# Second depthwise convolution of a selective-scan layer: tap split between three engines and order of its PSUM banks

## The reference

```python
xin = jnp.einsum('bchw,oc->bohw', x, in_proj_w)
xc = jax.nn.silu(_dwconv(xin, conv2d_w, conv2d_b))     # first depthwise 3x3
x1 = _dwconv(xc, dw_w, dw_b)                           # second depthwise 3x3
x1 = gelu(_layer_norm(x1 over channels, dw_ln_g, dw_ln_b))
offset = x1 @ off_w.T + off_b                          # 8 numbers a pixel
xd = _dcn_sample(xc, offset)                           # bilinear gather at the offsets
...                                                    # scan, layer norm, projection
```

## Time and profile before

| | |
|---|---|
| median of 3 runs | 2626.13 us |
| the profiled execution, its own time | 2632.59 us |
| its span | 2630.7 us |
| mean granted clock of TensorE | 0.934 |

### The profile page before, as it was taken

The page is one execution under the profiler, slowest core; times in us unless marked ns, Lnnn a source line. Parts: engine busy times, 40 slices in busy tenths (PEclk is TensorE's granted clock), DMA queues, the critical chain, the costliest instruction groups (busy, mean ns, idle before and its releaser), DMA issues.

```text
span 2630.7 us, 29183 instructions
## 1 busy us (share of the span) xinstructions
PE 2209.4 (84%) x7671; PEld 1139.9 (43%) x7671; DVE 1954.1 (74%) x3324; ACT 1457.5 (55%) x2268; POOL 1419.7 (54%) x1223
## 2 busy tenths in 40 slices
PE   3898769897978989986988977889899689899788
PEld 2397525343433333332335964454344233333233
DVE  6556746598967999994765667566889499999754
ACT  1743533485765676663346436237677466766532
POOL 2231019387857888872322400475778388888532
PEclk9988879899989999998997988899999799999989
DMA  4000463400000010014720008333000001001145
GB/s 175 1 1 0 150 215 105 167 1 0 0 1 1 17 33 17 16 33 122 236 46 1 0 1 288 117 104 128 0 0 1 2 1 32 17 21 29 51 119 120
DMA packets 131749, 155.96 MB, mean 59 GB/s; under 512 B 4951, under 2 KB 107743, under 8 KB 128247
## 3 DMA queue, kind: packets, MB, share of 16 engines
q1 hardware_dynamic: 131575, 154.00, 19.1%
HBM read 81.69 MB, written 72.29 MB: 59 GB/s over the span
## 4 chain that ended last, share of the span: by engine, by line
PE 42%; DVE 25%; issue 12%; POOL 8%; ACT 7%; DMA 3%; SPq 1%; DVEq 1%; ACTq 0%; POOLq 0%
PE PSUM L2190 7%; POOL BIG L900 6%; PE PSUM L701 6%; PE PSUM L2011 4%; DVE BIG L816 3%; DVE BIG L840 3%; PE PSUM L2246 3%; PE PSUM L2054 3%; PE PSUM L2252 2%; PE PSUM L2068 2%; PE PSUM L2210 2%; DVE BIG L847 2%; DVE PSUM L823 2%; DVE BIG L1082 2%; DVE BIG L861 2%
## 5 line engine op out<-in xcount | busy, mean ns | idle before, releaser
L900 POOL TENSOR_TENSOR BIG<-BIG 128x512 f32<-128x512 f32 x320 | 407.3, 1273 | 108.3 <-DVE BIG L861 86.1
L816 DVE TENSOR_TENSOR BIG<-PSUM,BIG 128x512 f32<-128x512 f32 x576 | 379.1, 687 | 74.1 <-PE PSUM L1010 31.1
L1082 DVE SCALAR_TENSOR_TENSOR PSUM<-BIG,VECS,PSUM 128x1024 f32<-128x1024 f32 x240 | 309.2, 1288 | 43.8 <-PE PSUM L2011 37.4
L742 POOL TENSOR_TENSOR BIG<-TOEP,BIG 128x384 f32<-128x384 f32 x84 | 97.2, 1183 | 342.7 <-DVE BIG L1484 342.7
L1010 PE MATMUL PSUM<-BIG,SELB 120*128 120x512 bf16 x576 | 211.6, 387 | 82.6 <-DVE BIG L816 74.7
L2011 PE MATMUL PSUM<-BIG,WDW 128*128 128x512 f32 x576 | 263.5, 604 | 11.3 <-ACT BIG L1920 11.3
L1718 POOL TENSOR_SCALAR BIG<-BIG,VECS 128x1024 f32<-128x1024 f32 x64 | 181.3, 2845 | 50.6 <-DVE PSUM L1542 50.6
L2190 PE MATMUL PSUM<-BIG 128*128 128x381 f32 (+1 forms) x576 | 190.1, 494 | 15.2 <-DVE BIG L749 15.2
L1016 PE MATMUL PSUM<-BIG,CSTS 128*128 128x512 f32 x384 | 202.4, 609 | 0.0
L1010 PEld LDWEIGHTS PSUM<-BIG,SELB 120*128 120x128 bf16 x576 | 56.0, 98 | 277.4 <-DVE BIG L816 185.1
L2011 PEld LDWEIGHTS PSUM<-BIG,WDW 128*128 128x128 f32 x576 | 108.2, 192 | 141.5 <-issue 126.9
(11 more groups left out here) (362 smaller groups left out, 5366.5 us busy)
## 6 DMA issues: line engine op xcount, KB each, us to landing
spill<-X SPq DMA_DIRECT2D x18, 1024.0 KB, 6.3
back_spill<-BIG SPq DMA_DIRECT2D x32, 576.0 KB, 3.4
X<-x SPq DMA_DIRECT2D x32, 512.0 KB, 7.6
rows_spill<-X SPq DMA_DIRECT2D x64, 256.0 KB, 4.2
out<-BIG SPq DMA_DIRECT2D x64, 256.0 KB, 3.6
BIG<-rows_spill SPq DMA_DIRECT2D x28, 512.0 KB, 5.1
X<-back_spill SPq DMA_DIRECT2D x14, 896.0 KB, 11.7
BIG<-fc SPq DMA_DIRECT2D x8, 1024.0 KB, 9.7
```

The lines of the kernel that those rows point to most:

```text
L742: eng.tensor_tensor(to.rearrange("p (x c r) -> p x c r", x=3, r=WROW), TOEP[:, y].unsqueeze(1).unsqueeze(1).broadcast_to([P, 3, WCH, WROW] ...
L816: dve.tensor_tensor(img(o), img(PSUM[:, (k + q) % 2, :]), pch(c, XBASE, dy, dx), ALU.mult).then_inc(df_p, 1)
L900: pool.tensor_tensor(XS[:, k, :], XS[:, k, :], product_buffer(q), ALU.add).then_inc(df_add, 1)
L1082: return dve.scalar_tensor_tensor(out=rows8(to), in0=strip(c, base, dy, dx), scalar=vc(weights, j), in1=rows8(acc), op0=ALU.mult, op1=ALU.add)
```

## The change

The nine taps are divided anew, and `d2_acc(c)` goes round three pairs of banks (0-1, 2-3, 4-5). GpSimd makes taps 4, 5 and 6, each with a multiplication and an addition of zero in one instruction, with two additions of two tensors; its `d_side` has two buffers. On even strips TensorE makes taps 7 and 8 and VectorE taps 0 to 3; on odd strips TensorE makes tap 8 and VectorE 0, 1, 2, 7 and 3. The centring is written back to the strip's own accumulator, and the offsets of strip c to the banks of strip c+1. VectorE now normalizes strip c-1 after the last tap of strip c and copies the offsets of c-3 before the later taps of c. TensorE makes the offsets of c-2 between centring and mean of c. ScalarE applies the Gelu of c-1 after the exponential of c. `d_xb` has one buffer.

```diff
-DW1_VECTOR, DW2_VECTOR = (4, 5), 6
-DW2_SIDE = (5, 6)
-DW2_FIRST = DW2_VECTOR - 1 + len(DW2_SIDE)
+DW1_VECTOR, DW2_VECTOR = (4, 5), (5, 6)
+DW2_TAPS, DW2_SIDE, DW2_FIRST = ((0, 1, 2, 3), (0, 1, 2, 7, 3)), (4, 5, 6), (7, 8)
+SIDE_STEPS = 2 * len(DW2_SIDE) - 1
...
-            return banks(2 * (c % 2))
-
-        IN, CEN, VAR = banks(6), banks(4), banks(6)
-        OFFS = PSUM[:, 6, 0:8 * 16].rearrange("p (r g) -> p r g", r=8)
+            return banks(2 * (c % 3))
+
+        IN, VAR = banks(6), banks(6)
+        def offs(c):
+
+            return PSUM[:, 2 * ((c + 1) % 3), 0:8 * 16].rearrange("p (r g) -> p r g", r=8)
...
                 def taps(c, first, last):
+                    n = DW2_VECTOR[c % 2]
...
-                        if j == DW2_VECTOR - 2:
-                            dve.wait_ge(d1_part, d2_side_done(pair_d2, c, 2))
-                            dve.tensor_tensor(d2_acc(c), d2_acc(c), d_side, ALU.add).then_inc(d2_tap, 1)
-                        elif j == DW2_VECTOR - 1:
-                            if c >= 2:
-                                dve.wait_ge(d2_cen, half_done(pair_d2, c - 2, 1))
-                            add_tap(dve, c, j - 1, XBASE, "dw_w", d2_acc(c), d_xb[:, c % 2, :]).then_inc(d2_tap, 1)
+                        if j == n - 2:
+                            dve.wait_ge(d1_part, d2_side_done(pair_d2, c, SIDE_STEPS - 1))
+                            dve.tensor_tensor(d2_acc(c), d2_acc(c), d_side[:, c % 2, :], ALU.add).then_inc(d2_tap, 1)
+                        elif j == n - 1:
+                            if c >= 1:
+                                dve.wait_ge(d2_cen, half_done(pair_d2, c - 1, 1))
+                            add_tap(dve, c, DW2_TAPS[c % 2][j - 1], XBASE, "dw_w", d2_acc(c), d_xb).then_inc(d2_tap, 1)
...
                 for c in range(NS):
-                    taps(c, 0, 4)
+                    taps(c, 0, 3)
+                    if c >= 3:
+                        offsets(c - 3)
+                    taps(c, 3, DW2_VECTOR[c % 2])
                     if c >= 1:
                         normal(c - 1)
-                    if c >= 2:
-                        offsets(c - 2)
-                    taps(c, 4, DW2_VECTOR)
                 normal(NS - 1)
+                offsets(NS - 3)
                 offsets(NS - 2)
                 offsets(NS - 1)
...
                 for c in range(NS):
-                    if c >= 1:
-                        pool.wait_ge(d2_tap, d2_taps_done(pair, c - 1, DW2_VECTOR - 2))
+                    if c >= 2:
+                        pool.wait_ge(d2_tap, d2_taps_done(pair, c - 2, DW2_VECTOR[c % 2] - 2))
...
-                    for to, j in zip((d_side, d_tap), DW2_SIDE):
+                    for n, j in enumerate(DW2_SIDE):
                         dy, dx = TAPS[j]
-                        pool.tensor_scalar(rows8(to), strip(c, XBASE, dy, dx), vc("dw_w", j), None, ALU.mult).then_inc(d1_part, 1)
-                    pool.wait_ge(d1_part, d2_side_done(pair, c, 1))
-                    settle(pool)
-                    pool.tensor_tensor(d_side, d_side, d_tap, ALU.add).then_inc(d1_part, 1)
+                        if n >= 1 and (c >= 1 or n >= 2):
+                            pool.wait_ge(d1_part, d2_side_done(pair, c, 2 * n - 2) if n >= 2 else
+                                         d2_side_done(pair, c - 1, SIDE_STEPS - 1))
+                            settle(pool)
+                        pool.tensor_scalar(rows8(d_tap if n else d_side[:, c % 2, :]), strip(c, XBASE, dy, dx), vc("dw_w", j),
+                                           cs("zero")[:, 0:1], ALU.mult, ALU.add).then_inc(d1_part, 1)
+                        if n >= 1:
+                            pool.wait_ge(d1_part, d2_side_done(pair, c, 2 * n - 1))
+                            settle(pool)
+                            pool.tensor_tensor(d_side[:, c % 2, :], d_side[:, c % 2, :], d_tap, ALU.add).then_inc(d1_part, 1)
...
                     act.preload_act_table_set("gelu_and_others")
-                    act.wait_ge(d2_y, strip_done(pair, c))
-                    act.activation(d_y[:, c % 2, :], d_y[:, c % 2, :], ACT.Gelu, bias=vc("dw_ln_b"),
-                                   scale=vc("dw_ln_g")).then_inc(d2_g, 1)
+                    if c >= 1:
+                        gelu(c - 1)
+                gelu(NS - 1)
...
-                    pe.wait_ge(d2_tap, d2_taps_done(pair, c, DW2_VECTOR - 1))
+                    pe.wait_ge(d2_tap, d2_taps_done(pair, c, DW2_VECTOR[c % 2] - 1))
+                    for h in range(2):
+                        half = slice(h * CH, (h + 1) * CH)
+                        pe.matmul(d2_acc(c)[:, half], cs("center"), d_xb[:, half], start=True,
+                                  stop=True).then_inc(d2_cen, 1)
                     if c >= 1:
                         pe.wait_ge(d2_y, strip_done(pair, c - 1))
-                    for h in range(2):
-                        half = slice(h * CH, (h + 1) * CH)
-                        pe.matmul(CEN[:, half], cs("center"), d_xb[:, c % 2, half], start=True, stop=True).then_inc(d2_cen, 1)
+                    if c >= 2:
+                        offsets(c - 2)
                     for h in range(2):
                         half = slice(h * CH, (h + 1) * CH)
                         pe.wait_ge(d2_sq, half_done(pair, c, h))
-                        if c >= 2 and h == 0:
+                        pe.matmul(VAR[:, half], cs("mean"), d_sq[:, half], start=True, stop=True).then_inc(d2_var, 1)
+                    if c + 2 < NS:
+                        if c >= 2:
                             pe.wait_ge(d2_o, strip_done(pair, c - 2))
-                        pe.matmul(VAR[:, half], cs("mean"), d_sq[:, half], start=True, stop=True).then_inc(d2_var, 1)
-                    if c >= 1:
-                        offsets(c - 1)
-                    if c + 2 < NS:
                         taps(c + 2)
-                pe.wait_ge(d2_o, strip_done(pair, NS - 2))
-                offsets(NS - 1)
+                pe.wait_ge(d2_y, strip_done(pair, NS - 1))
+                for c in (NS - 2, NS - 1):
+                    pe.wait_ge(d2_o, strip_done(pair, c - 1))
+                    offsets(c)
```

More of the change, by code:

```diff
@@ L140, in program @@
         WDW1 = sb("WDW1", [P, NTAP - min(DW1_FIRST), P])
-        WDW2 = sb("WDW2", [P, NTAP - DW2_FIRST, P])
+        WDW2 = sb("WDW2", [P, NTAP - min(DW2_FIRST), P])
         WL3 = sb("WL3", [P, 2, 2, P])
@@ L282, in program @@
         l2at = r.at
-        d_xb, d_rs, d_y = (r.take(2, STRIP) for _ in range(3))
-        d_sq, d_side, d_tap = (r.take(STRIP) for _ in range(3))
+        d_rs, d_y = (r.take(2, STRIP) for _ in range(2))
+        d_xb, d_sq, d_tap = (r.take(STRIP) for _ in range(3))
+        d_side = r.take(2, STRIP)
         r.at = l2at
@@ L1075, in d2_taps_done @@
         def d2_taps_done(pair, c, j):
-            return pair * (NS * DW2_VECTOR) + (c * DW2_VECTOR + j + 1)
+            before = sum(DW2_VECTOR[s % 2] for s in range(c))
+            return pair * (sum(DW2_VECTOR) * (NS // 2)) + (before + j + 1)
         def add_tap(dve, c, j, base, weights, acc, to):
@@ L1089, in d1_part_done @@
         def d1_part_done(pair, c, j):
-            return pair * (NS * 5) + (c * 2 + j + 1)
+            return pair * (NS * (2 + SIDE_STEPS)) + (c * 2 + j + 1)
         def d2_side_done(pair, c, j):
-            return pair * (NS * 5) + (NS * 2 + c * 3 + j + 1)
+            return pair * (NS * (2 + SIDE_STEPS)) + (NS * 2 + c * SIDE_STEPS + j + 1)
         @block.vector
@@ L1174, in _ @@
                     dve.tensor_copy(WMID[rows, q, b, :, cols], WCOL[rows, y, 1:3, :])
-            for w, name, first in ((WDW1, "conv2d_w", min(DW1_FIRST)), (WDW2, "dw_w", DW2_FIRST)):
+            for w, name, first in ((WDW1, "conv2d_w", min(DW1_FIRST)), (WDW2, "dw_w", min(DW2_FIRST))):
                 for j in range(first, NTAP):
@@ L1539, in taps @@
                             dve.wait_ge(d2_tap, d2_taps_done(pair_d2, c, j - 1))
[L1540 to L1546 removed]
+                        if j == n - 2:
[5 more added lines that the diff above has]
+                            add_tap(dve, c, DW2_TAPS[c % 2][j - 1], XBASE, "dw_w", d2_acc(c), d_xb).then_inc(d2_tap, 1)
                         else:
[L1548 removed]
+                            add_tap(dve, c, DW2_TAPS[c % 2][j], XBASE, "dw_w", d2_acc(c), d2_acc(c)).then_inc(d2_tap, 1)
                 def normal(c):
@@ L1553, in normal @@
                         dve.wait_ge(d2_off, strip_done(pair_d2, c - 2))
-                    dve.scalar_tensor_tensor(out=d_y[:, c % 2, :], in0=CEN, scalar=CENDW, in1=d_rs[:, c % 2, :],
+                    dve.scalar_tensor_tensor(out=d_y[:, c % 2, :], in0=d2_acc(c), scalar=CENDW, in1=d_rs[:, c % 2, :],
                                              op0=ALU.add, op1=ALU.mult).then_inc(d2_y, 1)
@@ L1558, in offsets @@
                     dve.wait_ge(d2_off, strip_done(pair_d2, c))
-                    dve.tensor_tensor(OFF[:, c * 8:c * 8 + 8, :], OFFS,
```

(12 more changed lines are left out.)

1 line of the change is left out of this document (removed).

## The result

The changed kernel takes 2611.39 us (median of 5 runs, 2606.39 to 2613.97) against 2626.13 us: a ratio of 0.9946, 95% interval 0.9929 to 0.9963, **14.7 us faster**. The profiled execution took 2606.4 us around a span of 2604.5; 2602 us was forecast, with 2594 to 2620 for the range. Run again beside the later experiments, it took 2609.4 us, ratio 0.9928 (0.9915 to 0.9941).

A forecast was written before the change was run, and what follows sets the result against it. A ring through several engines, 9.82 us a strip, was taken as the bound; with GpSimd pacing at 8.81, each pair of images saves 12.2 us, 24.4 in all: 2626.1 - 24.4 = 2602 us, range 2594 to 2620.

The forecast's parts named there:

- the main case: Whole kernel: the change does what the rows say and GpSimd paces; 2594 to 2612 us, chance 0.77.
- A ring of 9.82 us bounds the kernel now: Second depthwise convolution, steady part: a chain of waits through VectorE, TensorE and ScalarE repeats every 9.82 us a strip.
- Opening the ring alone wins at most 0.6 us a strip: Steady strips: waits along the ring are small, so more gain needs less work on VectorE and TensorE both.
- A product with two operations costs 1.20 us: GpSimd's products: multiply then add zero takes 1.20 us, against 2.845 us for the existing product.
- its rival's strip: GpSimd's products stay slow at 2.845 us: 13.74 us a strip, 2757 us in all, chance 0.10.
- GpSimd paces at 8.81 us: Steady strips after the change: GpSimd's three products and two additions set 8.81 us a strip against 9.82.
- TensorE costs 16.9 us in two strips: TensorE's centring, mean, offsets and taps after the change: 16.9 us in two strips, against GpSimd's 17.6.
- VectorE waits for GpSimd on even strips only, 0.3 to 0.6 us: Sign of being right: before the sum, VectorE waits for GpSimd on even strips only, 0.3 to 0.6 us.
- The end: From strip 15's sum and last tap to the last reduction of the first pair, put at 767.0 us.
- a slow centring: Stage's end: centring may again take 3.78 us because TensorE had idled; 1.3 us added for it.
- Interlocking orders: Rival, steady strips: each two strips lose another 1.0 us, period 9.3, 2618 us in all; chance 0.09.
- VectorE and GpSimd don't slow each other: Opposite of a rival: moved instructions cost the other engines what they save, nothing won, 2626 us, chance 0.04.

The follow-up runs named there:

- e2: Kernel before, with only GpSimd's two products given the two-operation form (multiply, add zero); 2625.93 us in one run beside 2626.45.
- e10: Kernel before with the new division of taps, old order and banks, two buffers for GpSimd's sum and one d_xb; 2644.4 us in one run.
- e3: Changed kernel with the old division of taps and old product form, so only order and banks new; 2615.0 us in one run, 2613.96 timed again.
- e1: Changed kernel with GpSimd's three products back to a single operation (multiply, no addition of zero); 2757.37 us in one run.
- e12: Changed kernel with every strip divided as the even ones (VectorE four taps, TensorE two, GpSimd three); 2609.65 us, ratio 0.9926.
- e6: Changed kernel with matmuls of zeros in TensorE's two idle stretches at the stage's end; 2602.06 us, ratio 0.9904.
- e9: Changed kernel with a new order and matmuls of zeros at the stage's end, plus 10 more before its first centring; 2595.32 us, ratio 0.9878.
- e4: Kernel before with the new division of taps, but old banks, old order and one buffer for GpSimd's sum; 2647.32 us in one run.

## Why the prediction was right, and where it was off

The forecast was 2602 us and the time 2611.39, so the gain was 14.7 us of 24.4. The mechanism in the steady part held; that the time still lies under 2612, the upper bound of the main case, is luck, since that bound stood for small waits in every strip and the loss came at the end.

- *A ring of 9.82 us bounds the kernel now.* Right: e2 and most strips of e10 keep 9.82 us with products of 1.20 us on GpSimd, e3 breaks it.
- *Opening the ring alone wins at most 0.6 us a strip.* Right for a steady strip, e3's 9.19 against 9.82, and VectorE's 9.21 was the bound as counted. Another 2.8 of e3's 11.7 us come from the first interval (8.3 us in place of 11.1), which I had not counted apart.
- *A product with two operations costs 1.20 us.* Right, 1.196, and its rival's strip was priced right (13.77 us, e1); its total was right in part by luck.
- *GpSimd paces at 8.81 us.* Right: 8.84 to 8.85; the 0.03 us more a strip are the wait before the third product, 0.21 us for 0.18. Middle forecast 15 x 8.81 = 132.2 us and VectorE some 1 us behind at its end, measured 133.1.
- *TensorE costs 16.9 us in two strips.* Too high; 16.1 by e3's rows (2 x 5.33 + 3.61 + 1.8). It changed nothing, because GpSimd is slower, but it let the alternation look necessary, which e12 shows it is not.
- *VectorE waits for GpSimd on even strips only, 0.3 to 0.6 us.* Right in the second pair, 0.64 us on strips 4 to 14, and on strips 12 and 14 of the first. Before that the first pair was catching up, an odd strip in 9.26 us and an even one in 7.80, without a wait. The sum of the first three strips waited as well (6.3, 1.1 and 1.2 us), which I had only for the first.
- *The end*: this is the step that was mis-sized. I put the reduction at 767.0 us, 17.5 us after the start of the last tap, with 1.3 us in it for a slow centring (3.78 - 1.98 would have been 1.8). It measured 24.4 and 20.7. TensorE waits 3.70 us for the last tap of strip 15, the granted clock falls to 1.2 GHz, and three or five groups of matmuls lie on the path at that clock, where the kernel before had one and parts of two. The gain of the stages was 14.4 us in place of 24.4. Of the 10 us missing, 6.9 + 3.2 are this end. e6 shows that they are the clock: with the same order and the clock kept up, its two ends take 34.4 us together, where I had forecast 35.0 and the changed kernel took 45.0. The prediction had the slow centring, 3.78 us, and its reason, that TensorE had idled; but the new order puts offsets and mean behind it on the path, and I went on costing those, and the two last groups, at the full clock. The page TensorE: Matmul & The Clock Gate of the Trainium skill (What's actually happening) says that the throttled state is the default and activity releases it. The ends without zeros agree: behind a wait of 2.8 us or more the same four instructions took 3.4 to 3.8 us in place of 2.0. The second end of e9 does not fit so simply.
- *The rivals.* Interlocking orders (2618 us, 16 above the forecast) did not happen in the middle; the 9 us lost came from another place. VectorE and GpSimd don't slow each other in these forms: 2357 ns an addition with both 94 to 95% busy.

## What to carry to other kernels

When a chain through all engines sets the period, first find in which queue a late result is asked for in front of independent work, and move it one step back; e3's order alone brought three quarters of the middle's gain and a time that can't be told from the changed kernel's, while moving work without it (e4, e10) made the kernel slower. Then give the last iteration an order of its own and look at TensorE's clock there: a pipeline that is deeper by one stage drains longer, and it drains while TensorE idles. Read the price of an instruction from a row of the same form, not of the same operation: adding zero made this one 2.4 times faster.
